# An attention and mixture-of-experts block: small subtractions change engine, and a GpSimd step changes place

## The reference

```python
mod = (_silu(L0_c) @ L0_wmod).reshape(8, 6, 1, -1)
sa, ca, ga, sb, cb, gb = (mod[:, i] for i in range(6))
ga = (2 * (ga >= 0) - 1) * jnp.maximum(jnp.abs(ga), 0.25)     # gb likewise
h = _layernorm(x) * (1 + ca) + sa
x = x + ga * attn(h)
h = _layernorm(x) * (1 + cb) + sb
x = x + gb * ffn(h)
```

```python
# attention: 16 heads of 16, latent size 64, causal
Q = (hidden_states @ Wq.T).reshape(b, t, h, d)
latent_k = hidden_states @ Wk_down.T
latent_v = hidden_states @ Wv_down.T
q_lat = jnp.einsum('bthd,hdl->bthl', Q, q_to_latent)
logits = jnp.einsum('bthl,bsl->bhts', q_lat, latent_k) / math.sqrt(l)
logits = jnp.where(causal, logits, -1e30)
attn = jax.nn.softmax(logits, axis=-1)
ctx_lat = jnp.einsum('bhts,bsl->bhtl', attn, latent_v)
heads = jnp.einsum('bhtl,hld->bthd', ctx_lat, v_up)
out = heads.reshape(b, t, h * d) @ Wout.T
```

## Time and profile before

| | |
|---|---|
| runs, median (lowest to highest) | 1156.96 us (1151.46 to 1160.07), 3 runs |
| profiled execution: time, span | 1156.82 us, 1155.1 us |
| mean granted clock of TensorE | 0.978 |
| busy: PE, VectorE, ScalarE, GpSimd | 96%, 75%, 51%, 55% of the span |
| the same in 240 to 260 us (attention) | 96%, 91%, 75%, 68% |
| distance of two even units (exponentials of heads (8, 0) and (10, 0)) | 44.06 us |

### The profile page before, as it was taken

The page is one execution under the profiler, slowest core; times in us unless marked ns, Lnnn a source line. Parts: engine busy times, 40 slices in busy tenths (PEclk is TensorE's granted clock), DMA queues, the critical chain, the costliest instruction groups (busy, mean ns, idle before and its releaser), DMA issues.

```text
span 1155.1 us, 21701 instructions
## 1 busy us (share of the span) xinstructions
PE 1112.3 (96%) x7482; PEld 865.4 (75%) x7482; DVE 861.1 (75%) x2213; ACT 594.1 (51%) x1083; POOL 633.1 (55%) x669
## 2 busy tenths in 40 slices
PE   9899999999999989999799999999999999999996
PEld 4555556656656668888688888888888888888886
DVE  4787888898898679889877677676777767777552
ACT  2356767877877653222253444544445444455441
POOL 4134566676675552232356656566565655666644
PEclk9789989999999999999999999999999999999998
DMA  7544557777767644876346554555545555455621
GB/s 198 91 99 101 115 120 182 178 147 179 187 131 177 208 160 109 270 220 164 98 139 165 134 131 123 155 140 134 134 127 153 134 143 136 119 152 132 168 58 19
DMA packets 100333, 165.44 MB, mean 143 GB/s; under 512 B 18424, under 2 KB 65016, under 8 KB 98176
## 3 DMA queue, kind: packets, MB, share of 16 engines
q1 hardware_dynamic: 83360, 137.04, 43.5%
q0 software_dynamic: 14336, 25.70, 11.5%
q10 hardware_dynamic: 2528, 1.32, 0.7%
HBM read 103.71 MB, written 34.11 MB: 119 GB/s over the span
## 4 chain that ended last, share of the span: by engine, by line
PE 63%; DVE 11%; issue 8%; POOL 8%; ACT 5%; DMA 3%; ACTq 1%; SPq 0%; DVEq 0%; POOLq 0%
PE MB L564 14%; PE LB L564 13%; PE LB L882 8%; PE MB L882 8%; PE UB L694 4%; PE LB L656 4%; PE UB L564 3%; PE XB L564 3%; POOL out_y L2001 3%; DVE junk L1337 2%; PE MB L633 2%; POOL XG L1966 1%; ACT P L1032 1%; ACT P L1034 1%; POOL HTl L1959 1%
## 5 line engine op out<-in xcount | busy, mean ns | idle before, releaser
L1959 POOL TENSOR_TENSOR HTl<-HF,HTh 128x512 fp32r<-128x512 f32 x156 | 217.6, 1401 | 207.7 <-ACT HTh L1095 207.4
L1337 DVE CUSTOM_DVE_ANT_0 junk<-MB,MK 128x256 bf16<-128x256 f32 (+3 forms) x512 | 218.6, 482 | 36.4 <-PE MB L633 35.5
L1863 POOL TENSOR_SCALAR_AFFINE_SELECT P<-P 128x256 f32<-128x256 f32 x256 | 101.3, 420 | 138.9 <-ACT P L1034 138.9
L2001 POOL DMA_INDIRECT out_y<-EO,IDX x64 | 108.7, 1699 | 75.7 <-DVE EO L1819 65.7
L1106 ACT ACTIVATE SIL<-LB,gbT 128x512 f32<-128x512 f32 x64 | 43.9, 686 | 191.8 <-PE LB L564 188.7
L1032 ACT ACTIVATE P<-LB 128x768 f32<-128x768 f32 x128 | 103.9, 812 | 73.4 <-PE LB L656 70.3
L633 PE MATMUL MB<-KS,QS 48*128 48x256 f32 (+3 forms) x512 | 132.8, 368 | 5.2 <-DVE NM L1337 3.4
L1095 ACT ACTIVATE HTh<-HF 128x512 fp32r<-128x512 f32 x156 | 97.8, 628 | 72.2 <-DVE HF L1709 72.2
L656 PE MATMUL LB<-QS,KS 50*128 50x256 f32 (+3 forms) x512 | 124.9, 358 | 3.5 <-ACT P L1032 2.6
L656 PEld LDWEIGHTS LB<-QS,KS 50*128 50x128 f32 x512 | 78.9, 190 | 50.2 <-issue 33.4
L633 PEld LDWEIGHTS MB<-KS,QS 48*128 48x128 f32 x512 | 81.7, 195 | 19.0 <-DVE NM L1337 12.7
(11 more groups left out here) (316 smaller groups left out, 3028.1 us busy)
## 6 DMA issues: line engine op xcount, KB each, us to landing
WR<-in_gw SPq DMA_DIRECT2D x16, 1024.0 KB
WR<-in_uw SPq DMA_DIRECT2D x16, 1024.0 KB
WR<-in_dw SPq DMA_DIRECT2D x16, 1024.0 KB
QS<-ST SPq DMA_DIRECT2D x96, 128.0 KB, 3.7
KS<-ST SPq DMA_DIRECT2D x90, 128.0 KB, 4.6
hD<-h SPq DMA_DIRECT2D x8, 1024.0 KB, 6.1
XT<-hD SPq DMA_DIRECT2D x7, 1024.0 KB, 8.3
X<-in_x SPq DMA_DIRECT2D x8, 512.0 KB, 5.2
```

The costliest lines, as they stand in the source:

```text
L1337: m = e.tensor_tensor_reduce(junk[:, o:o + w], MB[:, o:o + w], MK[:, 512 - w:512], 1.0, -3e38, ALU.add, ALU.max, NM[:, k // 4, 4 * (k % 4) ...
L1863: m = e.affine_select(out=dd, in_=dd, compare_op=ALU.is_ge, fill=0.0, base=0, pattern=[[0, 2], [1, 128]], channel_multiplier=-1)
L1959: e.tensor_tensor(HTl[:, slot, :], hf_of(n)[:], HTh[:, slot, :].bitcast(F32), ALU.subtract).then_inc(g_ht, 1)
L2001: e.indirect_dma_start(out=out2, out_offset=bass.IndirectOffsetOnAxis(ap=IDX[x_ % 3][:, q:q + 1], axis=0), in_=EO[:, q, :], in_offset=None ...
```

## The change

The subtraction NMl = NMf - NMh goes from VectorE to GpSimd, where it stands ahead of the masks of head 1 (second half) and of head 5 (first half of the next unit). Of the layer norms' sums, the negated mean and the variance plus epsilon go from VectorE to GpSimd, as two more products with constant tiles. The cast hh goes from VectorE to ScalarE for batch elements 1 to 7, behind the exponentials of heads 6 and 7 of odd units. The weights wo and gate are split by ScalarE (cast, step (0, 3)) and GpSimd (subtraction, step (0, 4)) and no longer by VectorE at steps (0, 5) and (0, 6). The gates are computed by three VectorE instructions in three steps, before by five in three. The second half of shift2 is issued at head 7, behind its masks, before at head 6. At the start SyncE issues the second half of the first K stack, before ScalarE; and the copy of the modulation rows stands ahead of the scaling of batch element 1. One transpose of batch element 2 uses the other PSUM bank.

```diff
...
-    halfc = at("halfc", 89216, [128, 4])
+    halves, shifts = at("halves", 89216, [128, 8]), at("shifts", 89408, [128, 8])
+    halfc, minus = halves[:, 0:4], halves[:, 4:8]
+    nm2, epsc = shifts[:, 0:4], shifts[:, 4:8]
     st2, mv2 = at("st2", 89248, [128, 4, 6]), at("mv2", 89344, [128, 4, 2])
-    rs2, nm2 = at("rs2", 89376, [128, 4]), at("nm2", 89408, [128, 4])
+    rs2 = at("rs2", 89376, [128, 4])
...
-            elif u:
+            else:
                 e.wait_ge(g_ks, 1)
             hs = slice(4 * half, 4 * half + 4)
 
-            for kind, dst in ((0, QS), (1, KS))[:2 if u else 1]:
+            for kind, dst in ((0, QS), (1, KS))[:2 if u or half else 1]:
...
-                    e.wait_ge(d_w, 4)
-                    e.wait_ge(d_gate, 1)
+                    e.wait_ge(g_w, 2)
...
-                        hT(b + 2, k - 5, ("hTa", "hTb")[k - 5])
+                        hT(b + 2, k - 5, ("hTa", "hTb" if old else "p1")[k - 5])
...
+        def upper(b, c):
+            e.wait_ge(a_hf, 2 * b + c + 1)
+            e.wait_ge(p_v, 2 * b)
+            e.activation(hh[:, c, :], hf[:, c, :], ACT.Copy).then_inc(a_hh, 1)
...
         def put_max(u, half):
             e.wait_ge(p_mt, 2 * u + half + 1)
             if u:
-                e.wait_ge(d_nm, 2 * u + half - 1)
+                e.wait_ge(g_nm, 2 * u + half - 1)
...
         def store_max(u, half):
             base = 64 * (u % 2)
-            e.wait_ge(d_nm, 2 * u + half + 1)
+            e.wait_ge(g_nm, 2 * u + half + 1)
...
-        def stack_k(half):
+        def stack_k():
 
             e.wait_ge(d_st, 2)
             e.wait_ge(g_ks, 1)
             for r, part in enumerate((0, 0, 1)):
-                e.dma_start(KS[r:48:3, 4 * half:4 * half + 4, :].bitcast(F32),
-                            ST[1][64 * half:64 * half + 64, part, :].bitcast(F32)).then_inc(c_stack[half], 16)
+                e.dma_start(KS[r:48:3, 0:4, :].bitcast(F32), ST[1][0:64, part, :].bitcast(F32)).then_inc(c_stack[0], 16)
+        def cast(done, dst, src):
+            e.activation(dst, src, ACT.Copy).then_inc(done, 1)
...
-        stack_k(0)
+        stack_k()
         qk(0, 1, 1, "p1")
-
-        e.wait_ge(c_stack[0], 96)
-        stack_k(1)
+        e.wait_ge(p_rows, 3)
+        e.activation(modS[:], LB[0:NB, :], ACT.Copy).then_inc(a_rows, 1)
         e.wait_ge(c_x[1], 16)
         scale1(1, 0)
         scale1(1, 1)
-        e.wait_ge(p_rows, 3)
-        e.activation(modS[:], LB[0:NB, :], ACT.Copy).then_inc(a_rows, 1)
         vproj(0, 0, "p0")
         vproj(0, 1, "p1")
         hT(1, 0, "p0")
+        upper(1, 0)
         hT(1, 1, "p1")
+        upper(1, 1)
         put_max(0, 0)
...
-                        hT(b + 2, k - 5, ("hTa", "hTb")[k - 5])
+                        hT(b + 2, k - 5, ("hTa", "hTb" if old else "p1")[k - 5])
+                    if k in (6, 7) and new2:
+                        upper(b + 2, k - 6)
+                if (u, k) == (0, 3):
+                    e.wait_ge(c_in, 80)
+                    cast(a_w, W["wo"][0][:].rearrange("p k n -> p (k n)"), wor[:])
+                    e.wait_ge(g_fill, 1)
+                    cast(a_w, GPh[:, :, 112:128], gr.rearrange("p (k n) -> p k n", k=2))
...
-        def moments(stt, mvt, rst, nmt, done):
+        def moments(stt, mvt, done):
             settled()
             for k in range(4):
                 m = e.bn_aggr(mvt[:, k, :], stt[:, k, :])
-            kept(m)
-            settled()
-            e.tensor_scalar(rst[:], mvt[:, :, 1], EPS, None, ALU.add)
-            e.tensor_scalar(nmt[:], mvt[:, :, 0], -1.0, None, ALU.mult).then_inc(done, 1)
+            m.then_inc(done, 1)
...
-        def put_max(u, half):
-            e.wait_ge(a_nm, 2 * u + half + 1)
-            if u:
-                e.wait_ge(c_nm[half], 32 * u)
-            e.tensor_tensor(NMl[half][:], NMf[half][:], NMh[half][:].bitcast(F32), ALU.subtract).then_inc(d_nm, 1)
...
-            if k == 4:
-                put_max(0, 0)
-            if k in (4, 5):
-                hT(1, k - 4)
...
-                if k == 0:
-                    put_max(u, 1)
-                if k == 4 and u + 1 < NU:
-                    put_max(u + 1, 0)
...
-                    kept(e.scalar_tensor_tensor(out=modA[:], in0=gates, scalar=-1.0, in1=gates, op0=ALU.mult, op1=ALU.max))
-                    kept(e.tensor_scalar(modB[:], gates, 0.0, 2.0, ALU.is_ge, ALU.mult))
+                    kept(e.tensor_scalar(modB[:], gates, 0.0, 0.5, ALU.is_ge, ALU.subtract))
                 if (u, k) == (0, 2):
                     settled()
-                    e.tensor_scalar(modA[:], modA[:], 0.25, None, ALU.max)
-                    kept(e.tensor_scalar(modB[:], modB[:], -1.0, None, ALU.add))
+                    kept(e.scalar_tensor_tensor(out=modA[:], in0=modB[:], scalar=4.0, in1=gates, op0=ALU.mult, op1=ALU.mult))
                 if (u, k) == (0, 3):
                     settled()
-                    e.tensor_tensor(gates, modA[:], modB[:], ALU.mult)
+                    e.scalar_tensor_tensor(out=gates, in0=modA[:], scalar=0.5, in1=modB[:], op0=ALU.max, op1=ALU.mult)
...
-        def moments(b, ready, rst, nmt, done):
+        def moments(b, ready, mvt, rst, nmt, done):
             e.wait_ge(ready, b + 1)
+            e.tensor_tensor(nmt[:], mvt[:, :, 0], minus[:], ALU.mult)
+            kept(e.tensor_tensor(rst[:], mvt[:, :, 1], epsc[:], ALU.add))
+            settled()
             kept(e.tensor_tensor(rst[:], rst[:], halfc[:], ALU.pow))
...
+        def put_max(u, half):
+            e.wait_ge(a_nm, 2 * u + half + 1)
+            if u:
+                e.wait_ge(c_nm[half], 32 * u)
+            e.tensor_tensor(NMl[half][:], NMf[half][:], NMh[half][:].bitcast(F32), ALU.subtract).then_inc(g_nm, 1)
...
+        def lower(n, dst, src, upper):
+            e.wait_ge(a_w, n)
+            e.tensor_tensor(dst, src, upper.bitcast(F32), ALU.subtract).then_inc(g_w, 1)
...
+        e.memset(minus[:], -1.0)
+        e.memset(epsc[:], EPS)
...
         hT(1, 1)
+        put_max(0, 0)
...
+                if k == 1:
+                    put_max(u, 1)
+                if k == 5 and u + 1 < NU:
+                    put_max(u + 1, 0)
                 main(u, k)
+                if (u, k) == (0, 4):
+                    lower(1, W["wo"][1][:].rearrange("p k n -> p (k n)"), wor[:],
+                          W["wo"][0][:].rearrange("p k n -> p (k n)"))
+                    lower(2, GPl[:, :, 112:128], gr.rearrange("p (k n) -> p k n", k=2), GPh[:, :, 112:128])
                 if not odd:
                     if k == 0 and old2:
                         outproj(b - 2, 1)
                     if k == 1 and old:
                         normalise(u - 2)
                     if k == 2 and old2:
-                        moments(b - 2, d_mv2, rs2, nm2, g_rs2)
+                        moments(b - 2, d_mv2, mv2, rs2, nm2, g_rs2)
+                    if k in (4, 7) and old2:
+                        shift2(b - 2, k // 7)
...
-                    if k in (4, 6) and old2:
-                        shift2(b - 2, k // 6)
...
```

More of the change, by code:

```diff
@@ L232, in block_program @@
     a_sil, a_ht, a_cut, a_xt, a_score = (sem(n) for n in ("a_sil", "a_ht", "a_cut", "a_xt", "a_score"))
[L233 to L236 removed]
+    a_sd, a_sc6, a_hh, a_w = (sem(n) for n in ("a_sd", "a_sc6", "a_hh", "a_w"))
+    (d_s, d_w, d_modT, d_mod, d_mv1, d_hh, d_st, d_mx, d_rec, d_tf, d_mv2, d_h2, d_lg) = (sem(n) for n in (
+        "d_s", "d_w", "d_modT", "d_mod", "d_mv1", "d_hh", "d_st", "d_mx", "d_rec", "d_tf", "d_mv2",
         "d_h2", "d_lg"))
@@ L1517, in vector_program @@
                         h2T(b - 2, 1, "h2b")
-                    if k in (6, 7) and new2:
-                        hT(b + 2, k - 6)
                     if k == 7 and old and new:
```

35 lines of the change are left out of this document (10 added, 25 removed).

## The result

| | before | changed |
|---|---|---|
| median of the runs (lowest to highest) | 1157.68 us, 4 runs beside the changed kernel | 1174.83 us (1171.46 to 1178.0), 4 runs |
| ratio to before, 95% interval | | 1.0162 [1.0123, 1.0201] |
| profiled execution: time, span | 1156.82, 1155.1 us | 1177.21, 1175.5 us |
| clock, whole span; 160 to 380 us | 0.978; 1.00 | 0.965; 0.95 |
| first exponentials of unit 8 to those of unit 10 ("pair 8/9") | 44.06 us | 47.59 us |

The changed kernel is 1.6% slower. The forecast was 1170 us, range 1145 to 1182, slower by over 1% with a chance of 0.50.

The account below looks back on a forecast made before the run. It took the chain of the maxima, a ring through ScalarE and GpSimd, as the bound. Pairs 12.6, units 12/13 2.8, units 14/15 1.2 and start -3.5 gave +13.1 on 1156.8: 1170 us, range 1145 to 1182.

Parts of the forecast that it names:

- The first place: Unit 8, head 1: ScalarE waits to issue for GpSimd's late maxima subtraction; 1.65 us, 2.2 with the cast.
- the cast: ScalarE's cast of hh for head 6 of odd units delays (7, 7) and GpSimd's run; 0.55 us.
- The second place: Unit 8, head 5: the subtraction behind the first half of shift2 comes late for ScalarE's issue; 1.2 us.
- The third place: Unit 9, head 1: TensorE's 0.80 us wait for masks goes, but work before the subtraction eats the gain; 0.
- The full pair: Two units like 8 and 9: 2.2 + 1.2 + 0 + 0.2 = 3.6 us longer, counted 3.5 times.
- The last units: Units 12/13, without a next cast, +2.8 us; units 14/15, where only the second place remains, +1.2 us.
- The start: Units 0 to 3: GpSimd is early, VectorE's relief counts and TensorE's 1.16 us wait goes; gain 3.5 us.
- VectorE's relief at nothing: VectorE loses about 3.5 us of work per pair, costed at nothing because another ring is longer.
- that ring: The ring through ScalarE and GpSimd, taken as longer than VectorE's and so setting the pair's time.
- The maxima are not late: Rival: the subtraction is written before ScalarE reaches the issue at unit 8, head 1; 1145 us, chance 0.17.
- The half absorption: Rival: ScalarE's 1.21 us idle before each unit's first exponentials absorbs part of the delay; 1160 us, chance 0.24.
- The clock rival: Rival: new stands bring lower-clock stretches, one in each of four pairs, about 2.3 us each; 1180 us, chance 0.12.

Follow-up runs that it names:

- experiment 5: The changed kernel with the casts of the upper h back on VectorE; 1168.74 us.
- experiment 2: The kernel before with only the maxima's subtraction moved to GpSimd; 1173.83 us.
- experiment 1: The changed kernel with the maxima's subtraction back on VectorE; 1157.76 us.
- experiment 3: The changed kernel with GpSimd's subtraction of the maxima one instruction group earlier, right behind the masks of heads 0 and 4; 1153.28 us.
- experiment 4: The changed kernel with ScalarE issuing the maxima's transfers one head later (heads 2 and 6, not 1 and 5); 1152.58 us.
- experiment 11: The changed kernel with each of GpSimd's subtractions of the maxima done twice in a row; 1187.29 us.
- experiment 6: The changed kernel with the second half of shift2 at head 6 again; 1174.95 us.
- experiment 7: The changed kernel with the maxima's subtraction on VectorE and ScalarE's issue one head later up to unit 12; 1162.91 us.
- experiment 8: The changed kernel with GpSimd's subtraction one group earlier and ScalarE's issue one head later up to unit 12; 1146.51 us.
- experiment 9: The changed kernel with ScalarE's issue one head later up to unit 12, and GpSimd's subtraction earlier only from unit 13 on; 1147.72 us.
- experiment 10: The kernel before with only ScalarE's issue of the maxima's transfers one head later up to unit 12; 1156.73 us.

## Why the prediction was right, and where its sizes were not

**The first place and the cast.** Predicted +2.2 us from (8, 1) to (8, 2); measured +2.25. GpSimd's run was pinned as described, the subtraction took 0.45 (estimated 0.4), and experiment 5 puts the cast at 0.43 (0.55; 0.49 is left between experiment 2 and the change). The spare time before the next exponentials was 0.91 - 0.6 = 0.3 us, not 0.35. Shown by experiments 1, 3, 4 and 11 from four sides.

**The second place.** Predicted +1.2, measured +1.14; it vanishes in experiments 3 and 4.

**The third place.** Predicted 0: 6.14 became 6.32 us, and experiment 6 gives no difference. The order of work by which the gain was eaten is the one traced.

**The full pair: the right sum, with a term missing and one too large.** Predicted +3.6, measured +3.53 in 8/9; the four pairs from unit 4 on grew by 1.48, 4.08, 3.53 and 3.37, together 12.5, where 12.6 was predicted. The two places give 3.39 as distances of exponentials. But I took a later exponential for a later TensorE, and the bound engine had work in hand: its stands in the pair (all over 0.12 us in its timeline, added) grew by 1.9 us only, from 1.05 to 2.99. The other 1.6 are about what 3.4 us at half speed can lose (at most 1.7; experiment 2 shows 1.1 in the unit). So the sum holds by luck: the clock, which stood in a rival and not in the sum, took the place of half a stand. One sees it in the steps too: +1.06 at (8, 3), in the low-clock stretch, and -0.92 in the others, where TensorE caught up.

**The last units, mis-sized.** Units 12/13: predicted +2.8, measured +6.9. Units 14/15: predicted +1.2, measured about +3.4 (exponentials of (14, 0) to the last of attention). Of the 6.9, unit 12 has 4.9, with the stand at head 1 and 6.8 us at 1.2 GHz, and unit 13 has 2.0. There the changed kernel had:

```profile
361.33 0.45 POOL L1859 TENSOR_TENSOR NMl<-NMf,NMh 16x128 fp32r<-16x128 f32 x1
...
361.80 0.51 ACTq L1031 DMA_DIRECT2D QS<-NMh  x1
362.34 2.05 ACTq L1031 DMA_DIRECT2D QS<-NMl  x1
...
365.87 0.38 PE L658 MATMUL LB<-QS,KS 50*128 50x256 f32 x1 [1.93 <-ACT P L1039]
```

The issue that I had taken from unit 8 as 0.6 us took 2.05 here, TensorE stood 1.93, and a stretch at 1.2 GHz from 367.2 us followed (step (13, 3) 4.99 us, before 3.49). Step (13, 1) grew by 2.24 us. Before, this issue took 0.61 us (at 347.09), so 1.44 of them are its length, and 0.80 are its later start: the first issue began 1.97 us behind the exponentials, before 1.17. In units 14/15 too a stand was followed by a stretch, 6.8 us from 401.3:

```profile
399.27 0.38 PE L658 MATMUL LB<-QS,KS 50*128 50x256 f32 x1 [1.47 <-ACT P L1039]
```

Over the traced kernels these two units take 49.1 to 49.6 us where no such stretch falls in them (before, experiments 1, 3, 7 and 8), 52.5 and 52.9 with 6.8 us of it (changed, 2) and 54.7 to 55.4 with 13.7 (5, 6 and 11). Experiments 9 and 10 lie between (52.6 and 50.0 with 10.2 and 3.4), and experiment 4, where TensorE waits for transfers, above (56.9 with 10.2). I carried one place's durations over to units whose neighbours differ, and left the clock out.

**The start, mis-sized.** Predicted -3.5: unit 0 began 2.3 us earlier, and unit 4 2.0. The wait of 1.16 us for the copy of v is gone, as predicted. From unit 0 on nothing was gained: units 0 to 3 took 91.3 us, before 91.0. TensorE stood 0.9 us less in them, but they hold 22.1 us at 1.2 GHz, before 16.2, which can hide VectorE's relief.

**The sum.** -2.0 + 12.5 + 6.9 + 3.4 = +20.8, against +20.4 measured between the two profiled spans. The predicted +13.1 had the pairs right, and the ends 7.8 short. The profiled execution is 2.4 us above the median, so the forecast of 1170 misses the median by 4.8.

**VectorE's relief at nothing.** Right for this kernel, where ScalarE's stand sets the pace. It stopped being right once that ring was cut: pair 42.26 in experiment 4, 43.79 in experiment 10 with the maxima on VectorE. So some 1.5 us a pair lay in the whole set of moves, hidden behind one wait; with the later issue and the maxima back on VectorE (experiment 7) it is not there (45.05).

**The rivals.** "The maxima are not late" did not meet its condition; experiment 4 shows that its gain was there (pair 42.26). The half absorption did not come: the 1.21 us that ScalarE idled before (8, 0) shrank to 0.18, with a cast of 0.66 us in them. The exponentials of (8, 0) start 0.5 us sooner behind those of (7, 7) than before, which gives back the first cast's delay and no more; the stand at (8, 1), behind it, was not touched. The clock rival came true in its mechanism, one stretch in each pair, and not in its time, since it was added to stands that were priced too high. What it took as its sign was weak: in unit 4 of the kernel before, TensorE had stood 0.33 and 0.41 us (151.09, 151.85) when the clock fell.

**What stays open.** The clock's part over the window is an account (up to 11.9 of the 18.9 us above), not a measurement. Experiment 3 removes the stretches from the window together with the stand, and experiment 4 those up to 350 us (6.8 us are left behind it); no edit removed the clock alone. What separates the two is the comparison of units 8 and 12 in experiment 2, of one execution.
